# A new order of the engines' work in a transformer block: loads on two queues, maxima by single banks, later parts and divisions

## What is computed

```
Xn = layernorm(X) * ln_g + ln_b
Q, K, V = Xn @ Wq + bq, Xn @ Wk + bk, Xn @ Wv + bv      (16 heads of 16)
A = softmax(Q K^T / 4, causal);  O = (A V) @ Wo + bo
x = layernorm(X + O)
h = relu(x @ W1 + b1);  alpha = softmax(h @ W2 + b2)    (8 experts)
y = sum_k alpha_k * U_k (V_k x)                          (rank 64)
out = layernorm(x + y)
```

## Time and profile before

| | |
|---|---|
| median of 3 runs | 595.31 us (594.9 to 597.22) |
| the profiled execution | 600.93 us |
| its span (first to last instruction) | 599.2 us |
| instructions | 6,944 |
| mean granted clock of TensorE | 0.864 |

### The profile page before, as it was taken

One profiled execution on the slowest core, in us unless ns is written; L12 is line 12 of the kernel. 1 busy time (PEld: TensorE's weight loads), 2 busy tenths in 40 slices (PEclk: granted clock), 3 DMA queues, 4 the chain that ended last, 5 costly groups with the idle time before them and its releaser, 6 DMA issues.

```text
span 599.2 us, 6944 instructions
## 1 busy us (share of the span) xinstructions
PE 451.5 (75%) x2352; PEld 211.2 (35%) x2352; DVE 317.9 (53%) x648; ACT 219.5 (37%) x478; POOL 87.7 (15%) x111
## 2 busy tenths in 40 slices
PE   0658626986869779999979568899879997853593
PEld 0343312422323433444435333434433433312253
DVE  7726338565537375754376286556487650041324
ACT  0221402632537145555534134345235464630110
POOL 9620300021121000301011010120000101010000
PEclk9986859777879779999989679699869999985688
DMA  4067782030221052434354020331001000010001
GB/s 141 0 76 100 97 217 30 12 47 12 35 33 18 5 75 57 54 49 58 42 66 89 10 40 16 66 50 20 2 1 52 4 16 4 17 50 9 0 0 35
DMA packets 24786, 25.57 MB, mean 43 GB/s; under 512 B 9264, under 2 KB 16176, under 8 KB 24752
## 3 DMA queue, kind: packets, MB, share of 16 engines
q1 hardware_dynamic: 24752, 25.13, 25.5%
HBM read 5.78 MB, written 2.10 MB: 13 GB/s over the span
## 4 chain that ended last, share of the span: by engine, by line
PE 56%; DVE 20%; DMA 8%; ACT 6%; SPq 4%; issue 3%; POOL 2%; POOLq 0%; DVEq 0%; ACTq 0%
PE ps L781 24%; PE ps L875 10%; DVE mx L684 10%; PE ps L855 10%; PE ps L828 7%; DMA o_t<-srow 5%; SPq L433 4%; ACT pr L556 3%; PE ps L796 2%; DVE st L591 2%; PE ps L834 2%; POOL qk L506 1%; DMA srow<-sums 1%; ACT qk L543 1%; DVE nv L601 1%
## 5 line engine op out<-in xcount | busy, mean ns | idle before, releaser
L556 ACT ACTIVATE pr<-ps 128x512 f32<-128x512 f32 (+3 forms) x384 | 167.4, 489 | 214.7 <-PE ps L855 213.3
L684 DVE TENSOR_REDUCE mx<-ps 128x2 f32<-128x1024 f32 (+3 forms) x160 | 175.8, 1115 | 97.2 <-PE ps L834 68.9
L855 PE MATMUL ps<-stq,stk 99*128 99x512 bf16 (+3 forms) x384 | 104.0, 355 | 14.4 <-ACT pr L556 7.3
L828 PE MATMUL ps<-stk,stq 96*128 96x512 bf16 (+3 forms) x384 | 98.4, 357 | 21.6 <-DVE mx L684 15.0
L875 PE MATMUL ps<-pr,va 128*32 128x512 f32 (+3 forms) x768 | 88.2, 534 | 11.8 <-POOL pr L515 11.7
L515 POOL TENSOR_SCALAR_AFFINE_SELECT pr<-pr 128x512 f32<-128x512 f32 x64 | 41.2, 646 | 345.3 <-ACT pr L556 345.3
L855 PEld LDWEIGHTS ps<-stq,stk 99*128 99x128 bf16 x384 | 25.7, 101 | 103.7 <-ACT pr L556 49.8
L828 PEld LDWEIGHTS ps<-stk,stq 96*128 96x128 bf16 x384 | 36.0, 105 | 56.3 <-DVE mx L684 23.4
L781 PE MATMUL ps<-w_o,o_t 128*128 128x256 f32 x64 | 21.3, 494 | 28.4 <-DVE o_t L720 28.4
L781 PE MATMUL ps<-xt,w_qk 128*128 128x512 f32 x64 | 38.1, 735 | 2.9 <-DVE mx L684 1.0
L781 PE MATMUL ps<-v_t,x_t 128*128 128x512 f32 x64 | 32.4, 634 | 2.3 <-DVE mx L684 2.3
(11 more groups left out here) (67 smaller groups left out, 340.7 us busy)
## 6 DMA issues: line engine op xcount, KB each, us to landing
stk<-qk SPq DMA_DIRECT2D x32, 96.0 KB, 2.8
stq<-qk SPq DMA_DIRECT2D x32, 96.0 KB, 2.8
x_in<-in_x SPq DMA_DIRECT2D x8, 256.0 KB, 3.0
stk<-qk SPq DMA_DIRECT2D x32, 64.0 KB, 2.8
stq<-qk SPq DMA_DIRECT2D x32, 64.0 KB, 2.8
o_t<-av_raw SPq DMA_DIRECT2D x16, 128.0 KB
o_t<-srow SPq DMA_DIRECT2D x16, 128.0 KB
out_y<-x SPq DMA_DIRECT2D x8, 256.0 KB, 2.3
```

The source lines that it names most:

```text
L556: nc.scalar.activation(probs(n, kt)[:, 2 * i + m, at0:], act_bank(ev)[:, at0:], ACT.Exp, scale=DH ** -0.5).then_inc(s_act_free, 1)
L684: nc.vector.tensor_reduce(dst, src, AX.X, ALU.max).then_inc(s_dve_free, 1)
L828: last = nc.tensor.matmul(banks[:, i, m * w:(m + 1) * w], stq[g][0:ROWS, 2 * i + m0 + m, tile(t % TPC)], stk[g][0:ROWS, k0 // CHUNK, 2 * i ...
L855: nc.tensor.matmul(bank[:, at0:], stk[g][0:ROWS + PARTS, kt // TPC, 2 * i + m, tile(kt % TPC)], stq[g][0:ROWS + PARTS, 2 * i + m, at0:], s ...
```

## The change

It rewrites the list of events and what depends on it:

- **Loads.** The query loads of batch 0's groups 0 and 1 are issued from ScalarE's queue, all others from SyncE's. Only chunk 0's loads of groups 0 and 1 stand right behind the first q/k products; group 2's come behind chunk 1's projection, group 3's behind "early", chunk 1's key loads at steps 3.3, 6.3, 9.3 and 12.3. Batch 1's keys of both chunks go by six DMAs a group, not twelve (`stk` and `qk` are laid out anew).
- **Start.** Chunk 0's layer norm, transposes and q/k products come before chunk 1's layer norm. `bo` (GpSimd adds the bias to x) moves to steps 6.1 and 8.1. All of block 0's maxima and all but one of block 1's come before step 0. The -1 rows of `stk` are written as fp32 words that hold two bf16 each.
- **Maxima.** A unit is one bank (four heads of 128 keys, two of 256, one of more): 11 units for a block of chunk 0, 27 for one of chunk 1. All of VectorE's ring goes bank by bank. "rows" stands three units behind its split. The course has six points in place of sixteen. Units are issued behind each of the four scores of a step, not behind each pair, and scores take their banks one by one.
- **Distances.** Inside the steps a part comes 14 events behind its qk (or before the load that needs it). Invert and back are at 3 steps and repeat at 4.5 behind a block's end, norm at 2.3 and 6.0, r1 at 6.3 and 6.8. `o_t` has a copy for each chunk, so "spread" waits for r1 of the batch before only. The 1/sqrt operations are a part of the layer norm of their own.
- **Last block.** Its values aren't sent by DMA: TensorE transposes them, VectorE multiplies by the reciprocals of the sums there, TensorE transposes back and ScalarE copies to `o_t` ("turn", "unturn").

```diff
     for t in range(chunk * TPC, (chunk + 1) * TPC):
         for k0 in range(0, (t + 1) * P, CHUNK):
             w = min(CHUNK, (t + 1) * P - k0)
-            n = 2 if w <= 2 * P else 1
-            units += [(t, k0, w, m, n, k0 + w == (t + 1) * P) for m in range(0, 2, n)]
+            n = 4 if w == P else 2 if w == 2 * P else 1
+            units += [(t, k0, w, j, n, k0 + w == (t + 1) * P) for j in range(0, HPG, n)]
...
+    for ev in order:
+        attention |= ev[0] == "score"
+        if ev[0] in ("kload", "qload"):
+            needed = [i for i, (_, p) in enumerate(waiting) if p[1] == ev[1] and p[4] == (ev[0] == "kload") and ev[3] in (p[3], None)]
+            if needed:
+                out += [p for _, p in waiting[:needed[-1] + 1]]
+                waiting = waiting[needed[-1] + 1:]
         out.append(ev)
+        if attention or ev[0] == "qk":
+            waiting = [(age + 1, p) for age, p in waiting]
+        while waiting and waiting[0][0] >= (14 if attention else 1):
+            out.append(waiting.pop(0)[1])
...
+        return [(at + 2.3, ("norm", b, c, 0)), (at + 6.0, ("norm", b, c, 1)), (at + 6.3, ("r1", b, c * TPC)), (at + 6.8, ("r1", b, c * TPC + 2))]
+
+    side = [(6.1, ("bo", 0, 0)), (8.1, ("bo", 0, 1))]
+    side += paced([(1.7, ("v", 0, t)) for t in (4, 6)], 0, 3)
+    side += paced(norm(1, 1, 0) + project(1, 0, ks) + norm(1, 1, 1) + project(1, 1, ks), 1, 9)
+    side += [(k, ("kload", 0, g, 1)) for g, k in enumerate((3.3, 6.3, 9.3, 12.3))]
+    side += paced([(1.7, ("qk", 1, m, c, 1)) for c in range(chunks) for m in ks], 9, 14)
...
+    order = [("load", 0, 0), ("weights", 0), ("load", 0, 1)] + [e for _, e in norm(1, 0, 0) + project(0, 0, ks)]
     order += [("qk", 0, m, 0, w) for w in (1, 0) for m in ks]
-    order += [(kind, 0, g, 0) for g in range(GROUPS) for kind in ("kload", "qload")]
-    order += [e for _, e in project(0, 1, ks)] + [("v", 0, 0), ("v", 0, 2)]
+    order += [("kload", 0, 0, 0), ("qload", 0, 0, 0)] + [("kload", 0, 1, 0), ("qload", 0, 1, 0)]
+    order += [e for _, e in norm(1, 0, 1) + project(0, 1, ks)] + [("v", 0, 0), ("v", 0, 2)]
+    order += [("kload", 0, 2, 0), ("qload", 0, 2, 0)]
...
-                due.append((issued + 2, needed.index(issued)))
+                due.append((issued + 3, needed.index(issued)))
...
-    course = [(0, needed[0] + 3)] + [(begins[n] - 3.5, needed[n] + 2) for n in range(2, blocks)] + [(len(track), len(todo))]
+    course = [(0, needed[1] - 1), (ends[0] - 2.5, needed[GROUPS] + 1), (ends[1] - 10.5, needed[2 * GROUPS - 1] + 1),
+              (ends[2] - 9, needed[3 * GROUPS - 1] + 1), (ends[2] - 2.5, needed[3 * GROUPS] + 1), (ends[3] - 10.5, len(todo))]
...
+    for w in (1, 0):
+        for m in ks:
+            order.append(("qk", 0, m, 1, w))
+            issue_max(issued + 3)
     issue_max(needed[0])
-    for c in range(1, chunks):
-        for w in (1, 0):
-            for m in ks:
-                order.append(("qk", 0, m, c, w))
-                issue_max(issued + 1)
-        order += [("kload", 0, g, c) for g in range(GROUPS)]
-    order.append(("early", 1))
+    rows_upto(0)
+    order += [("early", 1), ("kload", 0, 3, 0), ("qload", 0, 3, 0)]
+    issue_max(needed[1] - 1)
...
+            for behind, quarter, kinds in ((2, 0, ("drain", "spread")), (4, 0, ("invert", "back")), (5, 2, ("repeat",))):
+                if j == quarter:
+                    order += [(kind, n) for n in ended(k, behind) for kind in kinds if kind == "drain" or n < blocks - 1]
...
+    order += [("turn", blocks - 1), ("unturn", blocks - 1), ("r1", 1, TPC), ("r1", 1, TPC + 2)]
...
+            return ev[0] == "qload" and ev[1] == ev[3] == 0 and ev[2] < 2
...
-                pool.memset(stk[g][ROWS:ROWS + PARTS], -1.0).then_inc(s_stack_init, 1)
+                pool.memset(stk[g][ROWS:ROWS + PARTS].rearrange("p a c m s -> p (a c m s)").bitcast(F32), MINUS_ONE_TWICE).then_inc(s_stack_init, 1)
...
-                if dve_before[ev]:
-                    pe.wait_ge(s_dve_free, dve_before[ev])
+                if n_dve[ev] > DVE_RING:
+                    pe.wait_ge(s_dve_free, n_dve[ev] - DVE_RING)
...
+                if kind == "turn":
+                    n = ev[1]
+                    pe.wait_ge(s_drain, n + 1)
+                    bank = take_dve(ev)
+                    for i in range(TPC):
+                        last = nc.tensor.transpose(bank[:, tile(i)], av_raw[:, n % 2, tile(i)], ident[:])
+                    last.then_inc(s_dve_full, 1)
+                if kind == "unturn":
+                    bank = take_act(ev)
+                    pe.wait_ge(s_dve_free, n_dve["turn", ev[1]])
+                    for i in range(TPC):
+                        last = nc.tensor.transpose(bank[:, tile(i)], o_sb[:, i, :], ident[:])
+                    last.then_inc(s_act_full, 1)
```

More of the change, by code:

```diff
@@ L1 @@
+import struct
 from contextlib import ExitStack
@@ L66, in project, with norm @@
     return [(0.4, ("xt", b, c, k)) for k in ks]
+def norm(which, b, c):
+    return [(w, ("ln", which, b, c, part)) for part, w in enumerate((0.7, 0.7, 1.0, 0.5, 0.5))]
 def finish(b, c, ks):
[L72 to L80, removed]
+    return (norm(2, b, c) + [(0.5, ("x1t", b, c, k)) for k in ks]
+            + [(1.7, ("h", b, c, k)) for k in ks] + [(0.9, ("lg", b, c)), (0.2, ("weigh", b, c)), (0.9, ("alpha", b, c))])
 def mixture(b, c):
@@ L89, in mixture @@
         out += [(1.7, ("vx", b, t))] * (t in ts) + [(0.5, ("avt", b, t - 1))] * (t - 1 in ts) + [(1.7, ("u", b, t - 2))] * (t - 2 in ts)
[L90 to L93, removed]
+    third = norm(3, b, c)
+    return out + third[:4] + [(0.0, ("store", b, c, 0))] + third[4:] + [(0.0, ("store", b, c, 1))]
 def with_parts(order):
-    out, pending, age = [], None, 0
+    out, waiting, attention = [], [], False
     for ev in order:
-        if pending and ev[0] in ("kload", "qload"):
-            out.append(pending)
-            pending = None
+        attention |= ev[0] == "score"
[4 more added lines that the diff above has]
+                waiting = waiting[needed[-1] + 1:]
         out.append(ev)
[L105 to L108, removed]
+        if attention or ev[0] == "qk":
+            waiting = [(age + 1, p) for age, p in waiting]
+        while waiting and waiting[0][0] >= (14 if attention else 1):
+            out.append(waiting.pop(0)[1])
         if ev[0] == "qk":
-            pending, age = ("part", *ev[1:]), 0
+            waiting.append((0, ("part", *ev[1:])))
     return out
@@ L128, in program_order @@
[L128 to L133, removed]
@@ L134, in program_order @@
-    side += paced([(1.7, ("v", 1, t)) for t in (0, 2, 4, 6)], half + 0.05, half + 5)
[L135 to L139, removed]
+    ends = [begins[(i + 1) * GROUPS] for i in range(batches * chunks)]
@@ L140, in program_order @@
+    side += [(ends[1] + 14.0, ("load", 1, 1)), (ends[1] + 16.0, ("bo", 1, 1))]
+    side += output(1, 0, ends[2]) + paced(finish(1, 0, ks), ends[2] + 7, ends[2] + 16) + paced(mixture(1, 0), ends[2] + 16, ends[3] - 0.5)
+    side += [(ends[3] - 3.9, ("norm", 1, 1, 0)), (ends[3] - 0.6, ("norm", 1, 1, 1))]
     side.sort(key=lambda e: e[0])
-    order = [("load", 0, 0), ("weights", 0), ("load", 0, 1)]
-    order += [("ln", 1, 0, c, part) for c in range(chunks) for part in range(4)]
-    order += [("bo", 0, c) for c in range(chunks)] + [e for _, e in project(0, 0, ks)]
+    order = [("load", 0, 0), ("weights", 0), ("load", 0, 1)] + [e for _, e in norm(1, 0, 0) + project(0, 0, ks)]
@@ L195, in program_order @@
                     elif b + 1 < batches:
[L196 to L203, removed]
+                        order += [("kload", b + 1, g, None), ("qload", b + 1, g, 0)]
+            issue_max(int(target(k + (j + 1) / HPG)))
+            for behind, quarter, kinds in ((2, 0, ("drain", "spread")), (4, 0, ("invert", "back")), (5, 2, ("repeat",))):
+                if j == quarter:
+                    order += [(kind, n) for n in ended(k, behind) for kind in kinds if kind == "drain" or n < blocks - 1]
+            while side and side[0][0] < k + (j + 1) / HPG:
                 order.append(side.pop(0)[1])
@@ L524, in _ @@
                 kind, b = ev[:2]
+                if kind == "qload" and on_act_queue(ev):
+                    load_stack(act, ev)
                 if kind in ("xt", "x1t", "h"):
@@ L624, in _ @@
                     _, w, b, c, part = ev
-                    ts = [(i, c * TPC + i) for i in range(part % 2 * 2, part % 2 * 2 + 2)]
+                    if part == 2:
+                        make_rstd(w - 1)
+                    else:
+                        ts = [(i, c * TPC + i) for i in range(part % 3 * 2, part % 3 * 2 + 2)]
                     if part < 2:
```

237 lines of the change are left out of this document (126 added, 111 removed).

## The result

The changed kernel takes 547.64 us (median of 4 runs, 546.42 to 550.96), the kernel before 595.62 beside it: a ratio of 0.920, 95% interval 0.9155 to 0.9245, some 48 us less. The forecast was 531.5 us with a range of 502 to 568, so the direction and the range held and the gain was put 16 us too high. The profiled execution took 550.96 us, its span is 549.2, 50.0 us less than the span before.

A forecast was written before the change was run, and what follows sets the result against it. The prediction took TensorE to bound the middle, with 65.4 us of bubbles and a lowered clock, and order to bound both ends. Its terms summed to -63.8 us, from the median 531.5 us, range 502 to 568.

The forecast's parts named there:

- signs: Listed marks of a right forecast, such as o_t and select waits under 2 us and middle clock above 0.91.
- The start: Before the first drain: shorter memsets bring transposes 6.1 us earlier, ScalarE held by loads; 4 us gained, plus 12.9 for the hole.
- The hole's term: Near 74 us: batch 1's x loaded ahead of the key loads ends TensorE's wait for maxima, 12.9 us gained.
- The rival of the moved hole: Start doesn't get better, second queue adds little, group 3's loads come late: both start terms lost, 548 us; chance 0.14.
- Output projections: Middle: more distance from repeat's DMA to VectorE's o_t product closes three TensorE waits of 14.0 us; 13 gained.
- Parts: Middle: parts 14 events behind instead of 3 keep GpSimd free for causal selects; 10 of 11.7 us gained.
- Maxima: Middle: 144 added reduces cost 6 us on the path; finer banks and even issue gain 12 of 28.4 us.
- the level course: Middle: maxima issued at 3.3 to 4.2 units a step almost everywhere, credited with finer banks for 12 us gained.
- Tail: Last drain to projection: transposes instead of four DMAs take 3.8 us, not 13.7; 9.9 us gained.
- Clock: TensorE's middle, clock 0.89: fewer bubbles return 8 us of at most 40.
- VectorE as the bound: Rival: all 21.6 us of added reduces lie on the path, level course and clock give nothing; 567 us, chance 0.14.
- Slower through hand-overs: Rival: each added reduce costs 0.76 us with its hand-over to TensorE, 109 us in all; 646 us, chance 0.04.

The follow-up runs named there:

- u_queue: The changed kernel with all stack loads on SyncE's queue, none on ScalarE's: 0.918 of the kernel before, 547.7 us.
- x_r1: The changed kernel with the output projection one step later (7.3 and 7.8 behind the chunk): 0.909 of the kernel before, 543.6 us.
- u_parts: The changed kernel with the parts four events behind their q/k product instead of 14: 0.935 of the kernel before, 558.0 us.
- b_single: The kernel before with single-bank maxima alone, old order and course kept: 0.962 of the kernel before, 575.8 us.
- u_course: The changed kernel with the old uneven course of maxima from batch 0's second chunk on: 0.909 of the kernel before, 543.4 us.
- x_ln: The changed kernel with more distance between a layer norm's last part and its transposes: 0.909 of the kernel before, 543.2 us.
- u_tail: The changed kernel with the last block's division by four DMAs again instead of eight transposes: 0.931 of the kernel before, 556.1 us.
- x_both: The changed kernel with later output projection and more distance from layer norm to transposes, together: 0.889 of the kernel before, 531.8 us.

## Why the prediction was right, and where it was off

The range and the direction held, and both ends were right in their mechanism. The middle was not. Its terms come to 37 us, and 35 of them were to be waits that close (13, 10 and 12), but TensorE's idle time there fell by 2.4 us. What was closed at one place (select, rows, banks, some 18 us) opened at another (x and query loads, some 15). Of the signs, VectorE's blocked operations (end at 10.20 us), the maxima waits (14.5 us in the middle), the reduces' mean (655 ns) and the tail (3.0 us) came as they were put down. The waits for o_t (12.6 us) and for the select (5.4) are over 2 us, six stretches of TensorE before the last drain are over 3 us, 6.42 the longest, and the clock is 0.91, not above it.

*The start* was put at 4 + 12.9 us and the first drain came 20.8 us earlier. Undone, the memset costs 3 us (its interval doesn't part it from none) and the hole 7 by the ratio and 10 by the medians. The memset's working held to 0.3 us, and so did the reason why it would be worth less than 6.1: ScalarE was held, for 9.9 us rather than 7.8. The hole's term was mis-sized: it was read as a wait of 12.9 us and taken in full, though the order behind it has slack to make some of it up.

*The rival of the moved hole* fell, though its 548 us is what was measured: that is chance, since it got there by losing the start, which in fact gave 20.8 us. Its half on two queues was right: u_queue is the same without the second queue. That is the Trainium skill's rule (DMA: Bandwidth & Descriptors, Issuing engines are not separate DMA queues); the run agrees.

*Output projections, 13 us:* this step failed. 14.0 us became 12.6. The step compared repeat's distance with its landing alone. The changed kernel's timeline shows SyncE's queue at the worst of the three waits:

```profile
299.60 0.80 SPq L453 DMA_DIRECT2D stq<-mrow  x1
300.50 3.87 SPq L399 DMA_DIRECT2D stq<-qk  x6
304.41 0.62 SPq L474 DMA_DIRECT2D o_t<-srow  x1
...
311.87 0.69 DVE L743 TENSOR_TENSOR o_t<-o_t 128x512 f32<-128x512 f32 x1 [4.97 <-DMA o_t<-srow]
```

Repeat stands behind the rows' DMA, which waits for VectorE, and behind six query loads. Another wait, 4.07 us before the projection at 396.02, is of another kind: repeat was issued at 381.38, but VectorE came to the product only at 395.20, behind a split, the chain of 1/sqrt of the third layer norm, a reduce and a copy:

```profile
392.02 0.16 DVE L619 TENSOR_SCALAR nv<-mv 128x4 f32<-128x4 f32 x1
...
394.20 0.16 DVE L626 SCALAR_TENSOR_TENSOR rstd<-nv 128x4 f32<-128x4 f32 x1
394.39 0.69 DVE L704 TENSOR_REDUCE mx<-ps 128x1 f32<-128x512 f32 x1
395.00 0.27 DVE L727 CAST mrow<-ps 48x128 bf16<-48x128 f32 x1
395.20 0.67 DVE L743 TENSOR_TENSOR o_t<-o_t 128x512 f32<-128x512 f32 x1
```

The projection follows the product by a third of a step only, so TensorE stands through all of that. A step more (x_r1) brought 6 us (4 by the medians).

*Parts, 10 us:* u_parts costs 9 by the ratio, 10 by the medians. Right in the whole, though of the 11.7 us wait for the select 5.4 stayed.

*Maxima, +6 and -12:* mis-sized. Together they were put at 6 us gained; b_single, the banks alone, gains 23 (18 in the middle). The 6 us on the path was itself put too low by its own rule, as 28.4 of 65.4 times 21.6 is 9.4; no run shows a cost on the path at all. The reduces' busy time rose from 175.8 us to 188.5 in the changed kernel and 186.5 in b_single:

```profile
L704 DVE TENSOR_REDUCE mx<-ps 128x1 f32<-128x512 f32 (+3 forms) x304 | 188.5, 655 | 68.4 <-PE ps L863 37.2
```

```profile
L684 DVE TENSOR_REDUCE mx<-ps 128x1 f32<-128x512 f32 (+3 forms) x304 | 186.5, 655 | 77.9 <-PE ps L830 51.5
```

12.7 and 10.7 us, 88 and 74 ns for each of 144, not the 150 ns of the durations' difference. The durations themselves did grow by that much (304 x 655 ns against 160 x 1,115 is 20.7 us, 144 ns each), but neighbouring reduces overlap: 304 x 655 ns is 199.1 us, 10.6 more than the engine was busy. The Trainium skill's estimate, 18.0 us (Perfetto Trace Analysis, Optimizing Scalar/DVE Operations), is too high here as well. The same section's other remark, that breaking up instructions may help where the engine isn't saturated but makes bubbles elsewhere, agrees with b_single's 23 us. And the level course, which the forecast credited beside the banks, costs 6 us (4 by the medians) where u_course undoes it. It is also less level than the prediction says: in steps 37.5 to 55 it has 44 units, 2.5 a step.

*What the forecast left out:* the wait for normalised x, 1.4 us before and 12.2 after. The change spreads five layer norm parts over the steps and lets the transposes follow the last by as little, so they wait for VectorE where before they didn't. The forecast has no term for these transposes (xt and x1t) and did not ask what they stand behind. x_ln, which puts them further behind the layer norm, takes the wait to 1.3 us and gains 7 us by the ratio.

*Tail, 9.9 us:* 10.7 by the timeline (3.0 for 13.7), 10.8 by u_tail's stretch, 7 by its ratio. Right.

*Clock, 8 us:* 0.89 became 0.91. By 343.82 x 0.02 that is 7 us. The nearness to 8 is luck: the 8 had no working, and it was to come from fewer bubbles, while the idle time of the middle stayed at 61 us. The clock of one and the same order was 0.91 and 0.92 in the middles of the changed kernel and of u_tail, with busy times of 343.8 and 339.9 us, so 0.02 is only twice the scatter. That the busy time fell by 15.6 for this reason alone is not shown, nor why the clock rose.

*VectorE as the bound* fell: 254 of 405 us. *Slower through hand-overs* fell with b_single: VectorE's idle time before the reduces went down, from 97.2 us to 77.9 (68.4 in the changed kernel), with nearly twice as many.

## What to carry to other kernels

A bubble's price is not its length: of the parts undone one by one, the hole of 14 us cost 7 to 10, and in the middle waits of some 18 us were closed while its idle time fell by 2.4. Two waits that were closed by more distance gave 6 and 7 us alone and 18 together. Where an order is written by hand, check each moved event against what stands ahead of it on every queue that it crosses, SyncE's above all, and not only against its own latency. Grains of one PSUM bank instead of two were worth more than any one distance, at 74 to 88 ns of VectorE per added reduce.

## What was not expected of the hardware

An issue can block its queue for long. In the changed kernel 5 of 15 issues of `sums<-av_raw` took between 1.77 and 4.40 us; in the kernel before none of 16 was over 0.8. All five follow repeat's DMA, the 7 us one, by 1.3 to 4.1 us, as here:

```profile
328.32 0.62 SPq L474 DMA_DIRECT2D o_t<-srow  x1
329.04 0.54 SPq L461 DMA_DIRECT2D o_t<-av_raw  x1
329.62 4.40 SPq L462 DMA_DIRECT2D sums<-av_raw  x1
```

Here the issue ends at 334.02, 5.7 us behind the start of repeat's, and so it is with all five: 5.4 to 5.9 us. In u_queue, x_r1, x_both and u_course, which have five or six of them each, it is 5.4 to 6.0, however near the issue stood. Of the issues that came 5.5 us or more behind a repeat none was long, in the kernel before and b_single (16 issues each, none nearer than 5.8) as in the others. So this issue waits until repeat's DMA is some 5.4 us old; what it waits for inside isn't shown. In chunks with four steps to a block the change puts repeat of one block right ahead of the spread of the next, and what stands behind it in SyncE's queue waits with it.

Two queues slow each other. While ScalarE's queue issued 12 loads, 0.82 us each (9.89 in all), SyncE's issued 13 in 10.5 us, 0.81 each; alone, in u_queue, six took 3.76, 0.63 each. So both together issued a load every 0.42 us, one and a half times as many as one alone, not twice.
